# The token residual's base: transposed on TensorE, or loaded in token rows and scaled by VectorE

## The reference

```
g   = group_norm(x)                      # 32 groups
A   = softmax((Wq g + bq)^T (Wk g + bk)) # 2304 x 2304
x1  = x + gamma * (Wv g + bv) A^T + g * sigmoid(w2 relu(w1 mean(g)))
t   = x1 as 2304 token rows of 128
n   = layer_norm(t);   t = t + softmax(n n^T) n
u   = layer_norm(t);   t = t + top-2 of 8 experts of u, with gates
y   = t as an image
```

## Time and profile before

| | us |
|---|---|
| median of 3 runs | 2591.79 |
| profiled execution, its own time | 2592.6 |
| its span, first to last instruction | 2590.8 |
| TensorE busy | 2513.8 (97%) |
| VectorE busy | 2125.2 (82%) |
| ScalarE busy | 1817.5 (70%) |

### The profile page before, as it was taken

The page is one execution under the profiler, slowest core; times in us unless marked ns, Lnnn a source line. Parts: engine busy times, 40 slices in busy tenths (PEclk is TensorE's granted clock), DMA queues, the critical chain, the costliest instruction groups (busy, mean ns, idle before and its releaser), DMA issues.

```text
span 2590.8 us, 45244 instructions
## 1 busy us (share of the span) xinstructions
PE 2513.8 (97%) x15057; PEld 2309.5 (89%) x15057; DVE 2125.2 (82%) x6221; ACT 1817.5 (70%) x3550; POOL 450.1 (17%) x839
## 2 busy tenths in 40 slices
PE   6999999999999999999999999999999999999997
PEld 5889988899888999889998999889998899988996
DVE  6886788878888788887888878888779887898677
ACT  4767766677667776777767767667776677767775
POOL 0000221012210131101311013110140102301135
PEclk9999999999999999999999999999999999999999
DMA  1000000000000000000000000000000000000000
GB/s 39 1 19 1 4 11 1 22 4 7 7 1 23 4 7 7 23 1 4 10 4 22 1 4 10 4 22 1 4 10 4 22 1 4 13 1 4 1 10 13
DMA packets 11317, 23.10 MB, mean 9 GB/s; under 512 B 1360, under 2 KB 7760, under 8 KB 11088
## 3 DMA queue, kind: packets, MB, share of 16 engines
q1 hardware_dynamic: 11088, 20.20, 2.2%
HBM read 10.76 MB, written 9.44 MB: 8 GB/s over the span
## 4 chain that ended last, share of the span: by engine, by line
PE 80%; DVE 10%; ACT 5%; issue 3%; POOL 1%; DMA 0%; ACTq 0%; SPq 0%; DVEq 0%; POOLq 0%
PE ps L1168 22%; PE ps L1170 21%; PE ps L1169 21%; PE ps L1188 13%; DVE row_space L972 2%; ACT row_space L726 2%; PE ps L1313 1%; DVE pt_lo L1062 1%; DVE pt_lo L1067 1%; ACT row_space L778 1%; DVE pt_lo L987 1%; DVE xg_lo L932 1%; PE ps L1354 1%; ACT xg_hi L680 0%; PE ps L1353 0%
## 5 line engine op out<-in xcount | busy, mean ns | idle before, releaser
L737 ACT ACTIVATE pt_hi<-ps 128x384 fp32r<-128x384 f32 x864 | 419.2, 488 | 317.1 <-PE ps L1188 315.3
L987 DVE TENSOR_TENSOR pt_lo<-ps,pt_hi 128x384 fp32r<-128x384 f32 x864 | 474.3, 552 | 111.7 <-ACT pt_hi L737 104.8
L972 DVE TENSOR_SCALAR_CACHE_REDUCE row_space<-ps,key_bias 128x512 f32<-128x512 f32 (+1 forms) x720 | 493.1, 691 | 54.4 <-PE ps L1170 49.8
L1188 PE MATMUL ps<-ident,row_space 128*128 128x128 f32 x2736 | 447.3, 273 | 17.6 <-ACT row_space L726 17.6
L726 ACT ACTIVATE row_space<-row_space,negmax 128x512 f32<-128x512 f32 (+2 forms) x432 | 402.9, 933 | 57.6 <-DVE negmax L981 57.6
L1188 PEld LDWEIGHTS ps<-ident,row_space 128*128 128x128 f32 x2736 | 344.7, 141 | 101.5 <-ACT row_space L726 31.1
L1168 PE MATMUL ps<-pt_hi,v_hi 128*128 128x384 f32 x864 | 356.3, 412 | 8.3 <-ACT o_chan L746 7.6
L1067 DVE TENSOR_TENSOR pt_lo<-row_space,pt_hi 128x768 fp32r<-128x768 f32 x260 | 251.8, 969 | 92.2 <-ACT pt_hi L787 92.2
L778 ACT ACTIVATE row_space<-ps,shift 128x768 f32<-128x768 f32 x260 | 233.9, 899 | 131.0 <-PE ps L1170 126.4
L1168 PE MATMUL ps<-pt_hi,tn_hi 128*128 128x384 f32 x864 | 304.2, 352 | 7.4 <-DVE pt_lo L1067 6.0
L1170 PE MATMUL ps<-pt_hi,v_lo 128*128 128x384 f32 x864 | 293.2, 339 | 0.0
(11 more groups left out here) (206 smaller groups left out, 5375.6 us busy)
## 6 DMA issues: line engine op xcount, KB each, us to landing
x_chan<-x SPq DMA_DIRECT2D x24, 384.0 KB, 4.1
y<-acc SPq DMA_DIRECT2D x48, 192.0 KB, 1.9
t_tok<-eb SPq DMA_DIRECT2D x1, 516.0 KB, 5.9
t_tok<-ew SPq DMA_DIRECT2D x1, 516.0 KB, 6.7
row_space<-wqkv SPq DMA_DIRECT2D x1, 192.0 KB, 3.3
se_sb<-se SPq DMA_DIRECT2D x1, 68.0 KB, 5.3
biases<-channel SPq DMA_DIRECT2D x1, 2.0 KB, 5.6
```

The source lines that it names most:

```text
L737: act.activation(pt_hi[:, slot, :], ring_bank(step)[:, 0:BW], ACT.Copy)\
L972: dve.tensor_scalar(row_part(n, r, a, w), ring_bank(step)[:, 0:w], key_bias[:, row:row + 1], None, ALU.add, ALU.max, accum_out=mx[:, row % ...
L987: dve.tensor_tensor(pt_lo[:, slot, :], ring_bank(step)[:, 0:BW], pt_hi[:, slot, :], ALU.subtract).then_inc(pt_lo_ready, 1)
L1188: ins = pe.transpose(ring_bank(step)[:, k * 128:(k + 1) * 128], src(k), ident[:, :])
```

## The change

A second input, `tokens`, holds the same image in token rows (128 rows, 18 tiles, 128 channels). SyncE loads it straight into `t_tok`, in two pieces for each image (12 tiles and 6 tiles). The scale and shift are needed along the free axis now: VectorE spreads each over 128 columns (step `spread`), TensorE transposes both (step `rows`, 2 transposes), and ScalarE copies them to `base_rows`. Step `baset` is now two VectorE instructions of 128 x 384, a multiply and an add in place, the second behind a semaphore of the first. It has no part on TensorE or ScalarE, and one stands at slot 9 of every block. The three `base` calls of ScalarE are gone. The next image's load into `x_chan` waits for `xgnorm` in place of the last `baset`.

```diff
-BASE_TILES = {(1, 9): [0], (2, 10): [1], (3, 9): [2], (3, 12): [3], (4, 10): [4], (4, 12): [5]}
+BASE_TILES = {(1, 9): [0], (2, 9): [1], (3, 9): [2], (4, 9): [3], (5, 9): [4], (6, 9): [5]}
...
-         ('xgnorm', 0)], (6, 11): [('se_in',)], (6, 13): [('xgnorm', 1)], (6, 16): [('se_out',)], (6, 17): [('xgnorm', 2)]}
+         ('xgnorm', 0)], (6, 11): [('se_in',)], (6, 13): [('xgnorm', 1)], (6, 16): [('se_out',)], (6, 17): [('xgnorm', 2), ('spread',)]}
...
-                 16: [('base', 0)], 18: [('vproj', 2)], 19: [('vproj', 3), ('qproj', 1)], 20: [('vproj', 4), ('vproj', 5)],
-                 22: [('base', 1)], 35: [('base', 2)]}
+                 16: [('rows', 0)], 18: [('vproj', 2)], 19: [('vproj', 3), ('qproj', 1)], 20: [('vproj', 4), ('vproj', 5)]}
...
+            def load_tokens(b, u):
+                tiles = slice(0, 4 * TPB) if u == 0 else slice(4 * TPB, NT)
+                sp.dma_start(t_tok[:, tiles, :], tokens[b][:, tiles, :]).then_inc(tokens_loaded[u], 16)
+
+            sp.wait_ge(e_split, 2)
+            load_tokens(0, 0)
+            load_tokens(0, 1)
...
-                    sp.wait_ge(ring_full, filled(("baset", b, NB - 1)))
+                    sp.wait_ge(xg_norm_ready, at(xg_norm_ready, "xgnorm", b, LB - 1))
...
+                    sp.wait_ge(expert_added, at(expert_added, "expert", b, 3, TPB - 1))
+                    load_tokens(b + 1, 0)
+                    sp.wait_ge(o1_added, at(o1_added, "o1add", b, NB - 1))
+                    load_tokens(b + 1, 1)
                     store(b, 4)
...
-                elif kind == "base":
-                    u = step[2]
-
-                    act.wait_ge(xg_norm_ready, at(xg_norm_ready, "xgnorm", b, LB - 1))
-                    cols = slice(u * LW, (u + 1) * LW)
-                    act.activation(x_chan[:, cols], x_chan[:, cols], ACT.Identity, bias=yshift, scale=yscale)\
-                        .then_inc(base_done, 1)
+                elif kind == "rows":
+                    act.wait_ge(ring_full, filled(step))
+                    if b:
+                        act.wait_ge(base_tok_ready, at(base_tok_ready, "baset", b - 1, NB - 1))
+                    act.activation(base_rows[:, :, :], tiled(ring_bank(step)[:, 0:256]), ACT.Copy).then_inc(base_rows_ready, 1)
...
-                    act.activation(t_tok[:, TPB * m:TPB * (m + 1), :], tiled(ring_bank(step)[:, 0:BW]), ACT.Copy)\
-                        .then_inc(base_tok_ready, 1)
...
+                elif kind == "spread":
+                    if b:
+                        dve.wait_ge(ring_full, filled(("rows", b - 1, 0)))
+                    dve.tensor_copy(rows_src[:, :, :], gs[:, 9:11].unsqueeze(2).broadcast_to([128, 2, 128])).then_inc(rows_spread, 1)
...
+                elif kind == "baset":
+                    m = step[2]
+                    t = t_tok[:, TPB * m:TPB * (m + 1), :]
+                    shape = [128, TPB, 128]
+                    dve.wait_ge(base_rows_ready, at(base_rows_ready, "rows", b, 0))
+                    dve.wait_ge(tokens_loaded[m // 4], 16 * (b + 1))
+                    dve.tensor_tensor(t, t, base_rows[:, 0, :].unsqueeze(1).broadcast_to(shape), ALU.mult)\
+                        .then_inc(base_scaled, 1)
+                    dve.wait_ge(base_scaled, at(base_scaled, *step))
+                    dve.tensor_tensor(t, t, base_rows[:, 1, :].unsqueeze(1).broadcast_to(shape), ALU.add)\
+                        .then_inc(base_tok_ready, 1)
...
-                elif kind == "baset":
-                    m = step[2]
-                    pe.wait_ge(base_done, at(base_done, "base", b, m // 2))
-                    transpose3(step, lambda k: x_chan[:, m * BW + k * 128:m * BW + (k + 1) * 128])
+                elif kind == "rows":
+                    wait_ring(step)
+                    pe.wait_ge(rows_spread, at(rows_spread, "spread", b))
+                    for k in range(2):
+                        ins = pe.transpose(ring_bank(step)[:, k * 128:(k + 1) * 128], rows_src[:, k, :], ident[:, :])
+                    ins.then_inc(ring_full, 1)
```

More of the change, by code:

```diff
@@ L195 @@
 SOON = ("expert", "scaled", "vproj", "qproj", "score", "row_max", "gates")
-FIRST_BLOCK = {0: [('fold', 0)], 1: [('fold', 1)], 4: [('fold', 2), ('foldsplit',)], 5: [('base', 0)], 8: [('base', 1)],
-               9: [('base', 2)]}
+FIRST_BLOCK = {0: [('fold', 0)], 1: [('fold', 1)], 4: [('fold', 2), ('foldsplit',)], 5: [('rows', 0)]}
 def first_stage():
@@ L209, in first_stage @@
           ("score", 0, 0, 0, 4), ("row_max", 0, 0, 0), ("exp", 0, 0, 0, 0)]
-    rest = {8: [("gn_norm", 0)], 10: [("se_in", 0)], 13: [("se_out", 0)]}
+    rest = {8: [("gn_norm", 0)], 10: [("se_in", 0)], 13: [("se_out", 0)], 14: [("spread", 0)]}
     merge(rest, {j: [("vproj", 0, m)] for j, m in {6: 1, 7: 2, 8: 3, 10: 4, 12: 5}.items()})
@@ L266 @@
     "fold": ["ring_full", "bias_left"], "foldsplit": ["bias_folded", "e_hi_ready", "e_split"],
-    "xgnorm": ["xg_norm_ready"], "xg": ["xg_hi_ready", "xg_lo_ready"], "base": ["base_done"],
+    "xgnorm": ["xg_norm_ready"], "xg": ["xg_hi_ready", "xg_lo_ready"], "spread": ["rows_spread"], "rows": ["ring_full", "base_rows_ready"],
     "fuse": ["ring_full", "fused_hi_ready", "fused_ready"], "vproj": ["ring_full", "v_hi_ready", "key_bias_ready", "v_lo_ready"],
-    "baset": ["ring_full", "base_tok_ready"],
+    "baset": ["base_scaled", "base_tok_ready"],
     "qproj": ["ring_full", "q_hi_ready", "q_lo_ready"],
@@ L285 @@
 LAST = {"score": "score_ready", "s1": "p1_exp_ready", "o1evac": "o1_chan_ready", "o1half": "o1_chan_ready", "fold": "bias_left", "gn_dev": "gn_dev_ready", "gn_var": "gn_var_ready", "se_in": "se_hidden_ready", "se_out": "se_exp_ready",
-        "fuse": "fused_ready", "vproj": "v_lo_ready", "baset": "base_tok_ready",
+        "fuse": "fused_ready", "vproj": "v_lo_ready", "rows": "base_rows_ready",
         "qproj": "q_lo_ready", "pt": "pt_lo_ready", "ot": "o_added", "tnt": "tnt_lo_ready", "o1t": "o1_added",
@@ L340, with build @@
 RING_BANK, BANK_BEFORE = ring_banks()
-def build(nc, x, wqkv, channel, se, ew, eb, y):
+def build(nc, x, tokens, wqkv, channel, se, ew, eb, y):
     ctx = ExitStack()
@@ L373, in build @@
         t_tok = sb("t_tok", [128, NT, 128])
+        rows_src = sb("rows_src", [128, 2, 128])
+        base_rows = sb("base_rows", [128, 2, 128])
         t_late = sb("t_late", [128, 2 * TPB, 128])
@@ L455, in build @@
         xg_lo_ready = signal("xg_lo_ready")
-        base_done = signal("base_done")
+        rows_spread = signal("rows_spread")
+        base_rows_ready = signal("base_rows_ready")
+        base_scaled = signal("base_scaled")
+        tokens_loaded = [signal(f"tokens_loaded{i}") for i in range(2)]
         fused_hi_ready = signal("fused_hi_ready")
@@ L512, in build @@
         y_stored = [signal(f"y_stored{i}") for i in range(2)]
-        signals = {s.name: s for s in (score_ready, p1_exp_ready, o1_chan_ready, base_tok_ready, fused_ready, bias_left, expert_added, terms_ready, gn_dev_ready, gn_var_ready,
+        signals = {s.name: s for s in (score_ready, p1_exp_ready, o1_chan_ready, base_rows_ready, fused_ready, bias_left, expert_added, terms_ready, gn_dev_ready, gn_var_ready,
                                        logit_max_ready, o_added, o1_added, pt_lo_ready, q_lo_ready,
@@ L1388 @@
         "x": np.asarray(x).reshape(B, C, NTOK),
+        "tokens": np.asarray(x).reshape(B, C, NT, TILE).transpose(0, 3, 2, 1),
         "wqkv": np.stack([np.asarray(L0_conv_Wq), np.asarray(L0_conv_Wk), np.asarray(L0_conv_Wv).T], axis=1),
```

4 lines of the change are left out of this document (1 added, 3 removed).

## The result

| | before | after |
|---|---|---|
| median, us | 2592.03 (2591.48 to 2593.09) | 2616.53 (2616.38 to 2617.25) |
| ratio | | 1.0091, 95% interval 1.0079 to 1.0104 |
| span of the profiled execution, us | 2590.8 | 2615.5 |

Slower by 24.5 us. The forecast was 2604.5 with a range of 2588 to 2612: the sign was right, the size was not, and the time lies outside the range.

What follows compares the result with a forecast made beforehand. Both TensorE and VectorE fill blocks 1, 2 and 5, so whichever gets more work sets the time. Six images at +1.81 us, image 7 +1.44 and image 0 made 12.7 over the median 2591.79: 2604.5 us, range 2588 to 2612.

Steps and rivals of the forecast that it cites:

- The pair's price: At slot 9, the added multiply and add hold VectorE for 1.04 us; bounds 0.54 and 1.16.
- Blocks 2 to 5: Step changes of +1.04, -0.66, -0.66 and +0.68 us; the pair hidden in blocks 3 and 4, where TensorE sets the time.
- the cover of 0.36 us in block 5: Block 5's end: exponentials start 0.36 us after `negmax`, behind ScalarE's last `pt_hi`, so the pair costs +0.68 there.
- C: Rival: the pair isn't hidden in blocks 3 and 4, their idle time moves instead of shrinking; +27, 2632 us; 6%.
- D: Rival: every pair, in all blocks, is on the path and nothing is gained; +52, 2643 us; 4%.
- Rival A: TensorE binds in all blocks and VectorE's additions fit under it; -14.0, 2577.8 us; 10%.
- B: Rival: in the second attention, dropping ScalarE's three `base` calls removes TensorE's idle time; up to -16.5, 2588 to 2600 us; 10%.
- Block 6: No exponentials follow, but `pt_lo` run close ahead of the matmuls: +0.15 us, bounds 0 and 1.04.
- what goes from TensorE: Blocks 1 to 4: six groups of three transposes go, 0.33 us each; one each in 1 and 2, two in 3 and 4.
- Image 7: The last image, without `rows` and without a next image: +1.44 us.
- `rows`: Second attention: two transposes, two thirds of a group, on a full TensorE; +0.22 us.
- Image 0: First image, more slack on VectorE: +0.4 us; its first token load costs between 0 and 1.7 us, once.

Runs made afterwards that it cites:

- Experiment 4: Changed kernel with both instructions of the pair cut to 128 x 8, at the same places with the same semaphores: 2596.8 us, ratio 1.0018.
- experiment 7: Changed kernel, ring passing a bank, `rows` at slot 36, images 1 to 7's pairs at second-attention slots 50, 52 and blocks 3, 4, slots 9, 12: 2585.81 us.
- experiment 8: Changed kernel, ring passing a bank, `rows` at slot 36, pairs on VectorE at the earlier transposes' blocks and slots (block 4: 10, 12): 2607.53 us.
- Experiment 6: The kernel of experiment 5 with the pair moved from VectorE to GpSimd at the same places: 2581.81 us, ratio 0.9957.
- experiment 3: Changed kernel with `rows` at slot 36 of the second attention in place of slot 16: 2612.14 us, ratio 1.0078.
- experiment 9: Changed kernel with the pair on GpSimd, the ring of banks unrepaired and `rows` still at slot 16: 2594.03 us, ratio 1.0009.
- experiment 5: Changed kernel with each `baset` passing over one bank in images 1 to 6 and `rows` at slot 36: 2606.03 us, ratio 1.0048.
- experiment 1: Changed kernel with each `baset` step passing over one bank of the ring of seven in images 1 to 6: 2609.64 us, ratio 1.0069.
- experiment 2: Kernel before the change with its ring of seven turned by one bank at block 6's first `pt`, images 1 to 6: 2599.22 us, ratio 1.0030.

## Why the prediction was right and wrong

**The pair's price: right.** 1.05 us against the 1.04 worked out from the earlier trace rows. The size of one instruction and the 0.12 us extra for the one that waits both came from rows of like work. The Trainium skill's rule (VectorE: DVE Perf Modes, section The DRAIN you can't avoid), by which the wait is free, doesn't hold for this pair: the add, which waits, starts 0.58 us after the multiply, and what follows the add starts 0.47 after it. The same section says that a next instruction that isn't held starts earlier than that, before the pipe is empty; the 0.46 from which the prediction made 0.92 was such a step, so the rule and the row did not belong together. Blocks 2 to 5 came out within 0.05 us each: the bounds from idle time after slot 9 in the earlier trace rows, the cover of 0.36 us in block 5, and the hidden pairs of blocks 3 and 4 held. Experiment 4 confirms them for the single pairs. For a second pair the idle time after slot 9 is not enough: in block 4 it cost 0.27 us in experiment 7 and 1.46 in experiment 8, whose expectation missed it. Rivals C and D are out by blocks 3 and 4.

**Rival A is out, and B too.** Experiment 6 has TensorE relieved and VectorE as before, and still blocks 1 and 2 gained nothing: in images 1 to 7 only the groups of blocks 3 and 4 are a gain. There and in experiment 7 the long step is 186.03 and 186.04 against 186.00 without ScalarE's three calls, so their relief is worth nothing that shows; it may at most have paid for the two transposes of `rows` (forecast +0.22, measured about 0 once they wait for nothing).

**Block 6: the step that failed, 7.2 us of the gap.** The prediction took +0.15 for the pair's shadow there, with bounds of 0 and 1.04. The pair's part was in fact 0.23. The failure lies before it, in the step "what goes from TensorE": I counted the six groups' time and left out that they were six turns of the ring of banks. The bounds were drawn around the pair and could not hold +1.12 from another cause. The ring's rule stood in the code before the change, and the banks that the first matmul of the second attention waits for can be worked out from it on paper: before, key tiles 13 and 15; after, 14 and 17.
Image 7 is the counter-case that came for free. There key tile 17 had bank 1 before, among those awaited, and has bank 2 now: its block 6 fell by 0.61 us (17.99 to 17.38), where the forecast had no change. The other 0.5 us by which image 7 is below the forecast is its block 5, +0.16 against +0.68. Before the change VectorE was busy there for 22.3 of 26.04 us, in image 3 for 23.8; that this covers the pair is likely, but no experiment shows it.

**`rows`: mis-sized, 4.5 us.** +0.22 was the time of two transposes. The step also costs a wait for a bank in a ring of two: 0.9 us in all at slot 16 in each of six images, by experiments 3 and 9 (0.93 and 0.86). In the first second attention the experts' terms of an earlier image don't exist, the bank is free, and the step is +1.09, the pair of block 1 alone. Over the forecast that is 6 x 0.75 in the long step and next to nothing (0.05) in the first.

**Image 0: mis-sized, 1.6 us.** +0.4 against +2.09 at its first copy and -0.09 in its blocks. The token load was hidden: the multiply at 65.35 us had no wait before it, and both loads, issued from 58.84 us on, had landed after 4.0 to 4.7 us. 1.3 of the 2.09 are TensorE's clock; the other 0.76 is no more than the two profiles of the changed kernel differ by (81.12 and 80.36). Its granted clock in the changed kernel and, over the same time, in the kernel before (windows, columns as above):

```profile
77.00:80.50 3.50, 3.50 (x14) 3.12 (x15) 1.29 (x4) 2.14 (x4) 0.00 (x0) 0.54 0.00 0
```

```profile
77.00:80.50 3.50, 3.50 (x22) 2.94 (x21) 3.01 (x10) 3.39 (x8) 0.00 (x0) 1.00 0.00 0
```

0.54 of full on the mean, and 14 of TensorE's instructions in place of 22. From the last matmul ahead of TensorE's wait at the end of block 1 to the first copy it is 5.89 us, before 4.56; the stall itself is 1.48 us in both (1.32 of it shown as idle, the rest is the overlap of one matmul with the next).

**Sum of the gap.** 7.2 (block 6) + 4.5 (`rows`, with the first second attention) + 1.6 (image 0) - 1.1 (image 7) - 0.2 (blocks 2 to 5) = 12.0 us, all of the gap.

## What to carry to other kernels

A step taken out of a queue that hands out buffers in turn changes who holds which buffer for every step behind it, and a step put in takes one that may still be in use. Before costing such an edit, list for each fixed taker of a buffer (here the second attention's first matmul) whom it waits for before and after; it is a property of the order, needs no run, and was worth 6 x 1.12 + 6 x 0.9 = 12 of the 25 us here. Idle time on an in-order engine covers added work only if the work is queued in front of the wait: look where the longest gap stands, not how much idle time the block holds. And when work costs time on a full engine beside a nearly empty one, try the empty one before giving up the change: with the pair on GpSimd and both buffers put right it is 2581.8 us, with the pair on VectorE at slot 9 and the same repairs 2606.0, and with it on VectorE where that engine waits anyway 2585.8.

## What the hardware showed beside

**GpSimd and VectorE can hold each other up.** Experiment 6, image 3, block 6 (start, us, instruction):

```profile
1133.22 1.01 POOL L680 TENSOR_TENSOR t_tok<-t_tok,base_rows 128x384 f32<-128x384 f32 x1
1133.54 0.70 DVE L909 TENSOR_TENSOR gs<-gs 128x1 f32<-128x1 f32 x1
1134.17 0.67 DVE L942 TENSOR_SCALAR row_space<-x_chan,gs 128x768 f32<-128x768 f32 x1
1134.31 1.40 POOL L683 TENSOR_TENSOR t_tok<-t_tok,base_rows 128x384 f32<-128x384 f32 x1
```

L909 takes 0.15 us in the changed kernel (there L896, in the row above); started during GpSimd's multiply it takes 0.70 and ends with it, at 1134.24. GpSimd's add takes 1.01 us elsewhere; started during VectorE's L942 it takes 1.40, 0.39 more. Both come once in each of images 0 to 6. VectorE's `pt_lo`, one source of which is in PSUM, keeps its 0.55 us: 99 of them overlap GpSimd's pair, and none takes over 0.56. The Trainium skill (SBUF — State Buffer, section Who interferes with whom) states this: a VectorE instruction with two SBUF sources, or in a mode that uses two ports, and a GpSimd instruction that reads SBUF exclude each other, and whoever comes second waits in full. The trace agrees for L909, which ends within 0.01 us of the multiply. The add is 0.39 us longer, where L942 had 0.53 left; no row tells in which mode L942 runs. The skill also expects that moving work between these two might not help (Perfetto Trace Analysis, section Optimizing Scalar/DVE Operations); here it was worth 24.2 us (experiments 5 and 6), of which in their profiles 1.3 is the stretch at half clock told below. Why, the rows suggest: VectorE's stream in the full blocks is `pt_lo` and score copies out of PSUM, and block 6, where the 0.55 us were lost, has time for them (18.46 us, as before). GpSimd's pair takes 2.1 us; one of its instructions of 128 x 384 takes 1.01, its additions of 128 x 128 take 0.46.

**A stretch at half clock comes and goes with the execution.** Near 77 us TensorE's granted clock is 0.5 (1.2 GHz, the lower of its two levels) for 3.4 us in the changed kernel, in its second profile, and in experiments 1, 3 and 5; it is 1.0 there in the kernel before and in experiments 2, 4, 6, 7, 8 and 9. Experiments 5 and 8 have the same instructions in the same order up to slot 9 of block 2, at about 85 us, and the same last stalls before (0.44 or 0.45 and 1.48 us); one has the stretch, the other not:

```profile
77.40:80.80 3.40, 3.40 (x13) 3.02 (x12) 1.39 (x4) 2.25 (x4) 0.00 (x0) 0.50 0.00 0
```

```profile
76.30:79.70 3.40, 3.40 (x22) 2.97 (x21) 2.39 (x8) 3.16 (x7) 0.00 (x0) 1.00 0.00 0
```

(the first is experiment 5, the second experiment 8). So it isn't settled by the order of the instructions; TensorE's waits during the first 50 us differ by up to 0.6 us between the two. Nor is it pure chance, perhaps: the stall of 0.45 us stands only in the seven profiles with the full pair on VectorE in block 1, five of which have the stretch, and none of the five profiles without that stall has it. Whether the changed kernel meets it more often for this reason stays open, and 1.3 us with it. A second such stretch, 3.4 or 6.8 us long, stands in the last second attention of experiments 3, 5 and 6 and costs 1.3 to 2.8 us there; experiment 7 has the same stall of 2.2 us before it and no such stretch. Differences of 3 us between two versions are within what these stretches can do to one execution, which is why the steps, and not the medians alone, carry the readings above.
